# Stage 1 of a fused kernel: x0 of the tile in front moves between the two scans of the product

## What is computed

```python
ek, ekv = exp(min(k, 30)), exp(min(k, 30)) * v
nf, df = scan(a = a * decay + (ekv_t, ek_t))            # forward in time
nb, db = scan(same, reverse=True)                       # backward in time
euk = exp(min(u + k, 30))
num = nf + nb - ekv + euk * v
den = df + db - ek + euk
out = sigmoid(r) * (num / max(den, 1e-08)) * (0.8 + 0.2 * tf)
...
x = x + ffn(out)       # two rounds: logits, top-k, write, attention, rms norm
```

## Time and profile before

| | |
|---|---|
| median of 3 runs | 1136.23 us (1136.04 to 1138.14) |
| the profiled execution | 1136.02 us, its span 1134.2 us |
| mean granted clock of TensorE | 0.981 of full |
| busy share of the span | PE 93%, DVE 69%, ACT 52%, POOL 40% |
| stage 1 | up to about 395 us of the span |

### The profile page before, as it was taken

The page is one execution under the profiler, slowest core; times in us unless marked ns, Lnnn a source line. Parts: engine busy times, 40 slices in busy tenths (PEclk is TensorE's granted clock), DMA queues, the critical chain, the costliest instruction groups (busy, mean ns, idle before and its releaser), DMA issues. The chain is left out here.

```text
span 1134.2 us, 15697 instructions
## 1 busy us (share of the span) xinstructions
PE 1052.3 (93%) x5040; PEld 591.3 (52%) x5040; DVE 780.8 (69%) x1018; ACT 591.9 (52%) x972; POOL 452.0 (40%) x204
## 2 busy tenths in 40 slices
PE   4899999999999889989999999997889899999996
PEld 1344444444444432756666666664327466666663
DVE  6999999999999632456666665664224566666664
ACT  4788878787878610335555555555102333333332
POOL 7999999999999300001111111111000033333333
PEclk9999999999999989999999999998899999999998
DMA  3343434343343166943344354331669556868664
GB/s 134 130 148 130 140 125 146 131 148 131 134 145 111 64 253 279 338 134 130 112 148 153 111 173 143 114 111 56 250 254 354 181 186 222 288 234 288 234 221 148
DMA packets 83392, 196.54 MB, mean 173 GB/s; under 512 B 6802, under 2 KB 48914, under 8 KB 80276
## 3 DMA queue, kind: packets, MB, share of 16 engines
q1 hardware_dynamic: 83348, 195.97, 49.2%
HBM read 137.22 MB, written 58.73 MB: 173 GB/s over the span
## 5 line engine op out<-in xcount | busy, mean ns | idle before, releaser
L937 PE MATMUL bank<-work 128*128 (+1 forms) x1024 | 247.7, 386 | 7.9 <-PEq L515 4.8
L961 PE MATMUL bank<-work 128*128 (+1 forms) x512 | 232.0, 596 | 2.5 <-ACT work L1061 1.8
L375 PE MATMUL bank<-work,ident 128*128 128x512 f32 x384 | 192.1, 623 | 35.1 <-DVE work L304 35.1
L937 PEld LDWEIGHTS bank<-work 128*128 128x128 f32 x1024 | 189.5, 192 | 46.8 <-issue 25.8
L1106 POOL COPY xres<-work 128x1024 f32 (+1 forms) x32 | 33.3, 1041 | 369.1 <-DVE work L1043 369.1
L1116 POOL TENSOR_TENSOR work<-work 128x1024 f32<-128x1024 f32 x32 | 75.4, 2355 | 263.2 <-DVE work L1043 263.2
L961 PEld LDWEIGHTS bank<-work 128*128 128x128 f32 x512 | 97.7, 191 | 99.1 <-issue 92.9
L375 PEld LDWEIGHTS bank<-work,ident 128*128 128x128 f32 x384 | 66.1, 191 | 141.8 <-issue 97.4
L995 DVE TENSOR_TENSOR work<-bank,sbias 128x256 f32<-128x256 f32 x64 | 27.2, 425 | 147.3 <-PE bank L937 147.3
L296 DVE SCALAR_TENSOR_TENSOR work<-work,decay 128x512 f32<-128x512 f32 x128 | 124.4, 991 | 0.2 <-PE bank L375 0.2
L375 PE MATMUL bank<-work 128*128 128x511 f32 x256 | 121.8, 599 | 0.0
(11 more groups left out here) (153 smaller groups left out, 1469.1 us busy)
## 6 DMA issues: line engine op xcount, KB each, us to landing
work<-in_kT SPq DMA_DIRECT2D x32, 512.0 KB, 3.3
work<-in_xT SPq DMA_DIRECT2D x32, 512.0 KB, 3.3
x0T_scratch<-work SPq DMA_DIRECT2D x32, 512.0 KB, 2.6
work<-x0T_scratch SPq DMA_DIRECT2D x32, 512.0 KB, 4.0
x1T_scratch<-work SPq DMA_DIRECT2D x32, 512.0 KB, 2.6
work<-x1T_scratch SPq DMA_DIRECT2D x32, 512.0 KB, 4.9
work<-in_x_nat SPq DMA_DIRECT2D x32, 512.0 KB, 4.6
out<-work SPq DMA_DIRECT2D x32, 512.0 KB, 3.0
```

Source lines behind the costliest of these rows:

```text
L375: return nc.tensor.matmul(ps[:, at:at + n], w, v, start=start, stop=not start, skip_group_check=True)
L937: last = nc.tensor.matmul(ps_s[p], xTb[p][:, c, :], Amat[:, i, :, c * 32:c * 32 + 32], start=(c == 0), stop=(c == NC - 1))
L961: last = nc.tensor.matmul(ps_o[:, cols], attT[:, k * P:(k + 1) * P], Bmat[k][:, i, cols], start=(k == 0), stop=(k == 1), skip_group_check= ...
```

## The change

In the loop of VectorE the backward scan of the product, with its wait for the two half-products, moves ahead of x0 of the tile in front; the forward scan stays behind it. No other engine's stream changes.

```diff
@@ -324,6 +324,9 @@
                         wait(dve, num_ok, n)
                         half(gfv, ekv, d, prev_ok, od, ev)
                         half(gfv, ekv, d, prev_ok, ev, od)
+                    if n < NT:
+                        wait(dve, prev_ok, 2 * n + 2)
+                        backward(gfv, d2, gfv_ok)
                     if n > 0:
                         wait(dve, y_ok, n)
                         wait(dve, num_ok, n)
@@ -334,8 +337,6 @@
                         nc.vector.scalar_tensor_tensor(x0T, ps_num[:, :], g, den[1 - p], ALU.mult, ALU.mult)\
                             .then_inc(x0_ok, 1)
                     if n < NT:
-                        wait(dve, prev_ok, 2 * n + 2)
-                        backward(gfv, d2, gfv_ok)
                         forward(gfv, d2, gfv_ok)
                         wait(dve, sumk_ok, n + 1)
                         wait(dve, lg_ok, n - 1)
```

## The result

The changed kernel takes 1147.74 us (median, 1143.92 to 1149.67) against 1136.13 us (1133.44 to 1138.14) for the kernel before. The ratio is 1.0096, with a 95% interval of 1.0075 to 1.0117: slower by 8.5 to 13.3 us. The profiled execution is the lowest of its runs, 1143.92 us with a span of 1142.1.

The account below looks back on a forecast made before the run. VectorE, full but with 0.96 us of collisions per tile, was taken as the bound, TensorE nearly as long; after the change VectorE waits for TensorE. 0.11 + 9.6 + 0.83 = 10.5 us more gave 1146.7 us, range 1141 to 1155.

Parts of the forecast that it names:

- The loop: From x0 through TensorE, both product halves and the backward scan to the next x0: period 11.88 us against 11.55.
- Chain 7.61: TensorE's work from x0's end through euv sums, transposes, logits and product sums, without a gap: 7.61 us.
- v1: First half-product of the product on VectorE (L325), which waits for TensorE's product sums; record forecast about 1.05 us.
- X: The moment at which x0 (L334) ends on VectorE; the forecast counts each tile's times from it.
- The hold of 0.84 us: GpSimd's clamp L364 keeps VectorE's half-products from their SBUF operands for its first 0.84 us.
- v2: Second half-product of the product on VectorE (L326); forecast to fall from 1.52 to 0.74 us.
- the prediction's lower bound: Period of 11.57 us if the product halves meet no GpSimd hold at their new phase.
- The bubble of 0.11: Backward scan's wait right behind the second product half, formerly covered by x0: 0.04 + 0.07 = 0.11 us.
- Tiles 2 to 30: 29 x 0.33: Steady tiles of the stage, each forecast 0.33 us longer: 9.6 us in all.
- The whole-instruction hold: Rival: GpSimd keeps the way to L364's end; period 13.80 us, about 1202 us; chance 0.01.
- The old collision: Rival: first product half comes before L364, second still loses 0.78; period 12.35, about 1160 us; chance 0.09.
- No stall left: Rival: L364's hold ends before the product halves come; period 11.57, 1137.7 us, not slower; chance 0.08.

Follow-up runs that it names:

- the shorter chain: Changed kernel with TensorE's product sums right after the euv sums, ahead of x0's transposes and logits: 11.68 us a tile, 1142.79 us.
- the longer one in the old order: Kernel before with TensorE's transposes of x0 done twice, VectorE's order unchanged: 11.76 us a tile, 1145.03 us.
- the swapped halves: Changed kernel with the two product half-products in the other order, the even half first: 11.77 us a tile, 1145.4 us.
- the first place: Kernel before with the clamp of exp(-r) moved from GpSimd to VectorE, ahead of the first k half: 1151.48 us, ratio 1.0133.
- the second: Kernel before with the clamp of exp(-r) moved from GpSimd to VectorE, behind the euv product: 1126.96 us, ratio 0.9914.

## Why the prediction was right

It held as a whole: 1146.7 predicted, 1147.74 measured, slower by 10.5 forecast and by 11.6 found, in the range and with the mechanism named. The mechanism is confirmed tile by tile; that the totals lie only 1 us apart is partly luck, since the four executions after span 5.75 us.

- **The loop.** Chain 7.61 and hand-over 0.11 predicted for v1 at X + 7.72: 210.30 - 202.59 = 7.71. Idle about 0.76 us in each of 26 tiles, with TensorE as the releaser. Shown by the shorter chain (wait gone, 11.68) and the longer one in the old order (11.76).
- **The hold of 0.84 us**, taken from one row at the start of the kernel (where the prediction says "both read two SBUF operands", that fits VectorE's halves and L360; L364 reads one): L365 at X + 7.20 (7.19 predicted), v1's record 1.08 (1.05), v2's 0.74, the period 11.89 (11.88). Shown by leaving the clamp out (11.56, of which the prediction's lower bound was 11.57).
- **The bubble of 0.11**: 0.12 by the swapped halves.
- **Where the total is off.** From den of tile 1 to den of tile 31 the two traces differ by 357.14 - 345.56 = 11.58 us, and the prediction had 10.4 for that. The step at fault is "Tiles 2 to 30: 29 x 0.33". 28 of them took 0.345 each, but the first cost 12.67 - 11.61 = 1.06. In tile 2 after, GpSimd's k clamp (L355) still stood beside the euv product (L316), which took 2.05 instead of 1.22. VectorE thus came to the product halves 7.88 us after x0's end, without a wait for TensorE and ahead of L365, and met the clamp in the old way once more, 0.91 and 1.52 merged in the row below:

```profile
37.97 3.09 POOL L355 TENSOR_SCALAR work<-work 128x1024 f32<-128x1024 f32 x1
38.35 2.05 DVE L316 SCALAR_TENSOR_TENSOR work<-work 128x1024 f32<-128x1024 f32 x1
...
43.24 2.35 DVE L296 SCALAR_TENSOR_TENSOR work<-work,decay 128x512 f32<-128x512 f32 x2
43.58 3.20 POOL L365 TENSOR_SCALAR work<-work 128x1024 f32<-128x1024 f32 x1
```

  The last tile was 11.56 - 10.73 = 0.83, as predicted. Outside these tiles the two profiled executions, 7.9 us apart in all, don't add up to the medians: what stands before den of tile 1 was 2.2 us shorter after (the eight profiles with the clamp on GpSimd scatter there from 36.4 to 38.7 us whatever their order, so that is no effect of the change), and what comes behind the stage some 1.5 us shorter.
- **The rivals.** The whole-instruction hold would have given 13.80 in a tile: excluded, as 11.89 was measured. The rule of the Trainium skill that the prediction set beside it does not hold for VectorE's two-input half-products against GpSimd's one-input clamp in any run here. The old collision in the new order is what the shorter TensorE chain showed, only at 11.68 and not at 12.35, since VectorE then came early and not late. No stall left (11.57 in a tile) is what the kernel without the clamp gave, 11.56.

## What to carry to other kernels

An engine that is busy all the time can be paying for collisions inside its records. Compare one operation's duration in all its places before calling the engine the bound, and follow the value that is moved through every engine until it comes back: a moved step costs what stands in that loop, not what it costs on its own engine. When such a stall goes, look for the next loop with its length worked out. Here three lengths lay within 0.36 us of each other: GpSimd's loop with 11.53, VectorE's own work and stalls with 11.54, the loop through TensorE with 11.89. Of what was tried, only taking an instruction off GpSimd gave time back.

## What the runs showed of the hardware

A VectorE half-product, which has two SBUF inputs, waited for a GpSimd one-input instruction of 2.76 us only in that one's first 0.84 us. In stage 1 of the twelve profiles 123 half-products came 0.08 to 0.70 us after the start of such an instruction; less its own 0.74 us, each began 0.83 to 0.86 after that start. Another 536 came from 0.86 us on and took their 0.74 undisturbed; one at 2.76 waited, for the GpSimd instruction that followed. For a GpSimd two-input instruction of 2.36 us the wait ended at 2.15 to 2.22 (198 half-products). GpSimd's one-input instruction also got the port between two half-products that stood one behind the other: when v1 had ended, L364 held up v2.

The one-source clamp on VectorE, 1024 elements in 0.69 us when alone, behaved otherwise beside the same kind of GpSimd instruction. In 28 tiles it came 1.87 or 1.88 us after L357's start and took 1.43 to 1.45: in the tile shown it ended at 208.32, 0.55 us after L357 did (207.77). Less its own 0.69 us it began at about 207.63, 2.63 us into L357's 2.77. But in two tiles it came at 1.54 and 1.56, took 0.69, and L357 was stretched to 3.12 and 3.14. The Trainium skill, "SBUF — State Buffer", section "Who interferes with whom", has single-source `tensor_scalar` in a two-port mode hold or wait for the pair for a whole instruction. The 28 tiles look like that, the two tiles contradict it, and so do the half-products for the two-input form. An estimate from these rows: L357 held what the clamp needs from about 1.88 us (2.24, where the first of the two clamps ended, less the 0.36 by which L357 was stretched) to about 2.63 us after its start. Whether that is the writing of its result was not tried. In the late tile shown, coming 0.33 us sooner made the first place as good as the second, with a period of 11.36.
